# Latent attention: five or six of the sixteen block transfers of a unit issued from GpSimd, the reciprocals widened by a copy and transposed

## What is computed

```python
q = einsum('bld,dhk->blhk', xn, Wq)                 # 16 heads of 64
latent = einsum('bld,dc->blc', xn, Wkv_down)        # 64 wide
k = einsum('blc,chk->blhk', latent, Wk_up)
v = einsum('blc,chk->blhk', latent, Wv_up)
attn = softmax(where(causal, einsum('bqhd,bkhd->bhqk', q, k) / sqrt(64), -inf))
s = einsum('bqhd,hdo->bqo', einsum('bhqk,bkhd->bqhd', attn, v), Wout)
out = x + s * silu(two_layers(xn))
```

## Time and profile before

| | us |
|---|---|
| median of 3 runs | 2399.08 (2394.21 to 2402.8) |
| the profiled execution | 2381.4 |
| its span | 2379.5 |
| TensorE busy in the span | 2109.0 |
| VectorE busy | 1710.9 |
| ScalarE busy | 1339.7 |
| GpSimd busy | 999.0 |

### The profile page before, as it was taken

The page is one execution under the profiler, slowest core; times in us unless marked ns, Lnnn a source line. Parts: engine busy times, 40 slices in busy tenths (PEclk is TensorE's granted clock), DMA queues, the critical chain, the costliest instruction groups (busy, mean ns, idle before and its releaser), DMA issues. The chain is left out here.

```text
span 2379.5 us, 46754 instructions
## 1 busy us (share of the span) xinstructions
PE 2109.0 (89%) x16256; PEld 1663.6 (70%) x16256; DVE 1710.9 (72%) x3004; ACT 1339.7 (56%) x3178; POOL 999.0 (42%) x1081
## 2 busy tenths in 40 slices
PE   6579999999899899999998789888988898898986
PEld 4467777777677677777776667767766776776764
DVE  5587776777777977677763477786778687867783
ACT  3346666766466656666563565555554655455542
POOL 2475666656665657656562223112221222123211
PEclk8789999999899999999998899999999999999998
DMA  8343333333333433333323056775768666867675
GB/s 278 93 106 81 89 94 92 85 82 93 92 92 84 109 95 85 76 77 95 96 71 100 23 136 165 184 185 135 176 173 189 157 166 158 195 145 181 163 186 130
DMA packets 191589, 298.29 MB, mean 125 GB/s; under 512 B 52264, under 2 KB 97660, under 8 KB 190332
## 3 DMA queue, kind: packets, MB, share of 16 engines
q1 hardware_dynamic: 179068, 271.17, 45.2%
q10 hardware_dynamic: 12288, 24.13, 4.1%
HBM read 56.04 MB, written 20.97 MB: 32 GB/s over the span
## 5 line engine op out<-in xcount | busy, mean ns | idle before, releaser
L854 ACT ACTIVATE l_pp<-ps,l_mx 128x256 f32<-128x256 f32 (+1 forms) x512 | 228.4, 463 | 168.1 <-DVE l_mx L991 168.1
L2034 POOL TENSOR_TENSOR g_ctxu<-g_ctxu 128x256 f32<-128x256 f32 (+1 forms) x96 | 88.0, 917 | 550.9 <-ACT g_ctxu L1879 550.7
L1754 PE MATMUL ps<-g_turned,g_latV 128*64 128x256 f32 (+1 forms) x1984 | 289.0, 435 | 0.0
L1858 ACT ACTIVATE g_pt<-ps,g_mx 128x256 f32<-128x256 f32 (+3 forms) x256 | 200.9, 796 | 120.6 <-DVE g_mx L1952 71.1
L1858 ACT ACTIVATE g_pp<-ps,g_mx 128x128 f32<-128x128 f32 (+3 forms) x256 | 173.6, 688 | 166.3 <-DVE g_mx L1957 64.1
L1130 POOL TENSOR_TENSOR l_pp<-l_pp,l_rl 128x1024 f32<-128x1024 f32 (+1 forms) x128 | 230.1, 1798 | 87.4 <-DVE l_rl L999 87.2
L1981 DVE STREAM_TRANSPOSE g_bt<-g_pt 128x1024 f32<-128x1024 f32 (+1 forms) x176 | 191.6, 1123 | 59.5 <-DMA g_turned<-g_bt 39.7
L1754 PEld LDWEIGHTS ps<-g_turned,g_latV 128*64 128x64 f32 x1984 | 154.9, 146 | 74.1 <-issue 33.9
L1147 POOL TENSOR_TENSOR l_act_lo<-l_u,l_act_hi 114x512 fp32r<-114x512 f32 x96 | 126.1, 1314 | 163.0 <-ACT l_act_hi L904 162.8
L991 DVE CUSTOM_DVE_ANT_0 ps<-ps,l_mask 128x256 f32<-128x256 f32 (+1 forms) x512 | 188.4, 441 | 7.4 <-PE ps L703 7.4
L109 PE MATMUL ps<-l_h_hi,l_w_hi 128*114 128x512 f32 (+1 forms) x384 | 160.1, 417 | 25.8 <-DVE l_h_lo L1048 22.0
(11 more groups left out here) (200 smaller groups left out, 6211.1 us busy)
## 6 DMA issues: line engine op xcount, KB each, us to landing
l_pt<-l_bt SPq DMA_DIRECT2D x1024, 64.0 KB, 2.0
g_turned<-g_bt SPq DMA_DIRECT2D x320, 128.0 KB, 3.4
g_turned<-g_bt SPq DMA_DIRECT2D x320, 96.0 KB, 2.2
g_turned<-g_bt SPq DMA_DIRECT2D x224, 112.0 KB, 2.4
g_turned<-g_bt SPq DMA_DIRECT2D x224, 80.0 KB, 2.1
l_tab<-turns SPq DMA_DIRECT2D x64, 128.0 KB, 2.1
g_turned<-g_bt ACTq DMA_DIRECT2D x64, 128.0 KB, 4.4
g_turned<-g_bt SPq DMA_DIRECT2D x96, 64.0 KB, 2.0
```

Source lines behind the costliest of these rows:

```text
L854: act.activation(PP[:, i % NP, at, 0:n], ps[:, bank + a, jj * 2 * P:jj * 2 * P + n], ACT.Exp, bias=mx[:, g % 2, h, at:at + 1], scale=-1.0, ...
L1754: last = pe.matmul(o, latV[:, b % 2, c, :], turned[:, :, a, c, :, :], start=(c == 0), stop=(c == t), skip_group_check=True)
L1858: act.activation(to, both(k, a) if plan.apart(k) else scored(k, a)[0], ACT.Exp, bias=mx[:, u % 2, at:at + 1], accum_out=sm[:, u % 2, at:at ...
```

## The change

Three things are done, and then the order is planned anew.

1. A new table `BELOW` gives five transfers of a short unit and six of a long one to GpSimd, with semaphores sub0 and sub1 of their own. `ASIDE` (ScalarE) is two everywhere. So SyncE issues 9 of 16 in short tiles (12 before) and 8 of 16 in long ones (14 before).
2. `spread`, new on GpSimd, copies the reciprocals, each repeated 64 times, to the second half of `ctxu`, which is 256 or 512 columns. `weigh` transposes that half into PSUM, 2 or 4 transposes of 128x128, in place of the products with the identity. `share` waits for the spread two units back instead of the weighing.
3. All ranks and costs of the planner are new, so that all queues can come out in another order.

```diff
     LONG = NT // 2
-    ASIDE = (((0, 0), (1, 1), (2, 2), (3, 3)),) * LONG + (((0, 0), (1, 1)),) * (NT - LONG)
-    COST = (4.571, 3.923, 2.011, 2.809, 4.828, 5.535, 2.542, 5.643)
+    ASIDE = (((0, 0), (1, 1)),) * LONG + (((0, 0), (1, 1)),) * (NT - LONG)
+    BELOW = (((2, 2), (3, 3), (0, 1), (1, 2), (2, 3)),) * LONG + (((2, 2), (3, 3), (0, 1), (1, 2), (2, 3), (3, 0)),) * (NT - LONG)
+    COST = (2.709, 3.092, 3.306, 2.466, 4.391, 5.098, 3.285, 1.763)
     RANK = {
-        "pe": {"latent": -60.62, "values": -57.85, "query": -30.8, "scores": -17.92, "weigh": 10.13, "wout": 40.53,
-              "back": -13.38},
-        "act": {"split_x": -33.79, "latent": -163.61, "values": -36.79, "query": -27.04, "exp": 14.02, "evacuate": 14.31,
-              "gate": -17.61, "move": 17.17},
-        "dve": {"latent": -51.51, "query": -45.74, "largest": 6.21, "share": -103.46, "blocks": 19.74, "gate": 42.39,
-              "back": -18.9},
-        "pool": {"split_x": -49.69, "divide": 23.65},
-        "sp": {"xn": -39.07, "f": 41.91, "x": 19.24, "move": 22.1, "store": 39.09},
+        "pe": {"latent": -44.66, "values": -28.5, "query": 20.57, "scores": -25.24, "weigh": 9.27, "wout": 61.39,
+              "back": 36.22},
+        "act": {"split_x": -26.65, "latent": -41.17, "values": -25.91, "query": -23.27, "exp": -3.03, "evacuate": 3.82,
+              "gate": 49.96, "move": 8.11},
+        "dve": {"latent": 28.05, "query": -45.43, "largest": 9.61, "share": -17.89, "blocks": 22.83, "gate": -18.32,
+              "back": -21.63},
+        "pool": {"split_x": -50.02, "spread": -7.48, "divide": 22.69, "move": -19.14},
+        "sp": {"xn": -10.42, "f": -2.92, "x": 46.91, "move": 12.22, "store": 56.03},
     }
...
         if kind == "weigh":
             t = self.units[n][1]
             some = 1 if t == 0 else (t + 2) // 2 if event[2] == 0 else t + 1 - (t + 2) // 2
-            return 0.1 + some * (0.44 if t >= self.LONG else 0.91) + (0 if event[2] else 0.11 * self.size(n))
+            return 0.1 + some * (0.44 if t >= self.LONG else 0.91) + (0 if event[2] else 0.055 * self.size(n))
+        if kind == "spread":
+            return 0.25 + 0.00085 * self.size(n) * DH
         if kind in ("evacuate", "divide"):
             return (0.00166 if engine == "act" else 0.0051) * self.size(n) * P / 2 + (0.15 if engine == "act" else 0.55)
         if kind == "move":
-            aside = len(self.ASIDE[self.units[n][1]])
-            return 0.635 * (aside if engine == "act" else 16 - aside)
+            aside, below = len(self.ASIDE[self.units[n][1]]), len(self.BELOW[self.units[n][1]])
+            return {"act": 0.65 * aside, "pool": 0.53 * below, "sp": 0.635 * (16 - aside - below)}[engine]
...
                 if lead and event[2] == 0:
-                    out += [("sp", ("move", u - 2)), ("act", ("move", u - 2))]
+                    out += [(some, ("move", u - 2)) for some in ("sp", "act", "pool")]
         elif kind == "share":
             k = self.first[n + 1] - 1
-            out += [("act", ("exp", k, self.wide(self.units[n][1]) - 1))]
-            out += [("pe", ("weigh", n - 2, 1 if self.units[n - 2][1] else 0))] if n >= 2 else []
+            out += [("act", ("exp", k, self.wide(self.units[n][1]) - 1))] + ([("pool", ("spread", n - 2))] if n >= 2 else [])
+        elif kind == "spread":
+            out += [("dve", ("share", n))] + ([("pool", ("divide", n - 2))] if n >= 2 else [])
         elif kind == "move":
             k = self.first[n + 1] - 1
             out += [("dve", ("blocks", k, 1 if self.long(k) else 0))]
             out += [("pe", ("weigh", n - 2, 1 if self.units[n - 2][1] else 0))] if n >= 2 else []
         elif kind == "weigh":
             b, t, r = self.units[n]
-            out += [("sp", ("move", n)), ("act", ("move", n)), ("act", ("values", (b * NT + t) // TZ)), ("dve", ("share", n))]
+            out += [(some, ("move", n)) for some in ("sp", "act", "pool")] + [ ("act", ("values", (b * NT + t) // TZ)), ("pool", ("spread", n))]
...
+        def below(u):
+            return sum(len(plan.BELOW[units[v][1]]) for v in range(u % 2, u + 1, 2))
+
         def moved(u):
-            return 16 * (u // 2 + 1) - kept(u)
+            return 16 * (u // 2 + 1) - kept(u) - below(u)
...
                     for i in range(4):
                         for j in range(4):
-                            if (i, j) not in plan.ASIDE[units[u][1]]:
+                            if (i, j) not in plan.ASIDE[units[u][1]] + plan.BELOW[units[u][1]]:
                                 sp.dma_start(PT[32 * j:32 * j + 32, u % 2, i, 0:run(u)],
                                              BT[32 * i:32 * i + 32, u % 2, j, 0:run(u)]).then_inc(s[f"pt{u % 2}"], 16)
...
                     if i == 0:
                         pe.wait_ge(s[f"pt{u % 2}"], 16 * moved(u))
                         pe.wait_ge(s[f"own{u % 2}"], 16 * kept(u))
+                        if below(u):
+                            pe.wait_ge(s[f"sub{u % 2}"], 16 * below(u))
                         pe.wait_ge(s["v"], tile(u)[0] + 1)
-                        pe.wait_ge(s["rl"], u + 1)
+                        pe.wait_ge(s["spread"], u + 1)
                         n = plan.size(u) // 2
-                        for h in range(2 * n):
-                            at = bank * CH + (n + h // 2) * P
-                            pe.matmul(flat[64 * (h % 2):64 * (h % 2) + 64, at:at + P], rl[:, u % 2, h:h + 1].to_broadcast([P, DH]),
-                                      ident[:, :], start=True, stop=True, skip_group_check=True)
+                        for j in range(n, 2 * n):
+                            at = bank * CH + j * P
+                            pe.transpose(flat[:, at:at + P], ctxu[:, u % NCU, j * P:(j + 1) * P], ident[:, :])
...
                 def share(u):
                     dve.wait_ge(s["ex"], heads[first[u + 1]])
                     if u >= 2:
-                        dve.wait_ge(s["pv"], u - 1)
+                        dve.wait_ge(s["spread"], u - 1)
                     own = slice(0, plan.size(u))
                     dve.reciprocal(rl[:, u % 2, own], sm[:, u % 2, own]).then_inc(s["rl"], 1)
...
                     if u >= 2 and p == 0 and a == 0:
                         dve.wait_ge(s[f"pt{u % 2}"], 16 * moved(u - 2))
                         dve.wait_ge(s[f"own{u % 2}"], 16 * kept(u - 2))
+                        if below(u - 2):
+                            dve.wait_ge(s[f"sub{u % 2}"], 16 * below(u - 2))
...
+                def spread(u):
+
+                    pool.wait_ge(s["rl"], u + 1)
+                    if u >= NCU:
+                        pool.wait_ge(s["clo"], u - NCU + 1)
+                    if u == 0:
+                        pool.wait_ge(s["cut"], 4)
+                    n = plan.size(u)
+                    pool.tensor_copy(ctxu[:, u % NCU, n * DH:2 * n * DH].rearrange("p (h d) -> p h d", h=n),
+                                     rl[:, u % 2, 0:n].unsqueeze(2).to_broadcast([P, n, DH])).then_inc(s["spread"], 1)
+
...
+                def move(u):
+
+                    pool.wait_ge(s["blocks"], heads[first[u + 1]])
+                    if u >= 2:
+                        pool.wait_ge(s["pv"], u - 1)
+                    for i in range(4):
+                        for j in range(4):
+                            if (i, j) in plan.BELOW[units[u][1]]:
+                                pool.dma_start(PT[32 * j:32 * j + 32, u % 2, i, 0:run(u)],
+                                               BT[32 * i:32 * i + 32, u % 2, j, 0:run(u)]).then_inc(s[f"sub{u % 2}"], 16)
+
                 for e in plan.program["pool"]:
```

More of the change, by code:

```diff
@@ L1233, in __init__ @@
             events[kind] = [(kind, z) for z in range(Z)]
-        for kind in ("evacuate", "divide", "move"):
+        for kind in ("evacuate", "spread", "divide", "move"):
             events[kind] = [(kind, u) for u in range(U)]
@@ L1272, in rank @@
             return self.start[n] + at
-        if kind in ("share", "weigh", "evacuate", "divide", "move"):
+        if kind in ("share", "spread", "weigh", "evacuate", "divide", "move"):
             return self.start[self.first[n + 1] - 1] + at
@@ L1544, in attend_g @@
         tri = ctxu[:, 0, 0:4 * P].rearrange("p (k n) -> p k n", k=4)
-        late = "x_in f_in silu clo latlo v qlo ex ev wo prod back y out".split()
+        late = "x_in f_in silu clo latlo v qlo ex ev wo prod back y out sub0 sub1".split()
         past, last = ({n: sem for n, sem in s.items() if (n in late) == some} for some in (False, True))
@@ L2047, in _ @@
                         forget(pool, over)
+                    elif e[0] == "spread":
+                        spread(e[1])
                     elif e[0] == "divide":
                         divide(e[1])
+                    elif e[0] == "move" and plan.BELOW[units[e[1]][1]]:
+                        move(e[1])
                 pool.wait_ge(s["clo"], len(units))
@@ L2081, in build @@
```

(2 more changed lines are left out.)

## The result

The changed kernel takes 2428.28 us in the median (2423.44 to 2431.25, 4 runs), the kernel before 2397.23 (2394.21 to 2402.8, 4 runs): a ratio of 1.0125, with a 95% interval of 1.0098 to 1.0152. It is slower by 1.25%; I had forecast 2337, faster by 2.6%.

The account below looks back on a forecast made before the run. It took SyncE's issuing queue, beside TensorE, to bound the last stage. Terms 34 + 12 + 27 + 4 - 15 = 62 us less, carried over to the 2399.1 us median, gave 2337 us, range 2285 to 2400.

Parts of the forecast that it names:

- SyncE's queue as the bound: Last stage: SyncE's issuing, 93% occupied, bounds beside TensorE; with fewer issues it falls under 60% and stops being a bound.
- the loop is 7.9 to 8.6 us: Last stage: a long unit's SyncE issues plus landing take this long after the change, shorter than any unit time.
- rival B: Tiles 6 and 7: the DMA engines bound units at their present 11 us, only other units gain; 2363 us, chance 0.17.
- The order planned anew: Queue orders under new ranks: effect unreadable from the trace, taken as 0 with plus or minus 15 us.
- TensorE's work, 42 less 8 us: Weigh: 256 transposes replace 1024 products, saving 42 us, less 8 us not of use in tiles 6 and 7: 34.
- The waits for transfers, 27 us less: TensorE before weigh: 27 of the 37.6 us of waiting for landed transfers would go.
- VectorE's waits: VectorE: most of 32.1 us at the share reciprocal and 45.4 us before g_bt goes; 12 us counted through score banks.
- rival D: GpSimd's queue: its issues cost far more than SyncE's, filling it from about 1.24 us each; 2447 us at 1.4, chance 0.15.
- the 15 us that I charged for a busy GpSimd: GpSimd's queue: 15 us added for pieces of TensorE's work that find it busy, some 0.15 us in each of 96 units.
- Rival C: Last stage: idle time only moves, GpSimd's queue replaces SyncE's as what weigh awaits; 2399 us, no change, chance 0.08.
- rival A: Last stage: the forecast itself, SyncE's queue no longer a bound, TensorE nearer its own work; 2337 us (2285 to 2375), chance 0.60.

Follow-up runs that it names:

- e8: The changed kernel with only its planner told the measured SyncE time of a move by tile and a landing of 3.2 us: 2356.1 us, ratio 0.9846.
- e14: The whole change with measured planner prices and a second set of newly searched ranks: 2324.4 us, ratio 0.9689 to the kernel before.
- e6: The kernel before with half the columns of each block sent from unit 24 on, same number of issues: 2376.21 us, ratio 0.9921.
- e15: The kernel before with measured planner prices and newly searched ranks and spacing: 2366.1 us, ratio 0.9865.

## Why the prediction was wrong, point by point

*SyncE's queue as the bound.* The step that failed is "a long unit takes 8 x 0.69 = 5.5 us of queue", and with it "the loop is 7.9 to 8.6 us". In the medians over batches 1 to 3, SyncE's eight issues for a unit of tile 7 stretch over 7.9 us, and the first product comes 11.4 us after the first issue; in e8 and e14, whose orders don't wait for it so much, 12.5 and 13.6. Until the last block has landed it is 10.3 us in tile 6 and 10.7 in tile 7. As the price of one issue on a queue that issues nearly alone, 0.69 us was right, as e6 shows (0.66 and 0.68 us with half the bytes). I carried it over to three queues at once, where the bytes bound the unit and the slot becomes 1.02 and 1.10 us. The rows had a better estimate for tile 7: 195 GB/s at a busy share of 0.83 make 235 GB/s, at which 2.10 MB take 8.9 us, and with the shortest landing of 1.8 us 10.7 us. This is an estimate, and for tiles 4 to 6 it is too low: 7.4, 8.5 and 9.6 us, where 9.1, 10.3 and 10.3 were measured. In rival B I gave such a bound 0.17. For the kernel before it is not true, since with half the bytes e6 has hardly shorter units there. In the changed kernel the bytes do bound a unit's arrival, but not its time at 11 us, as B had it: e14, with the same transfers in another order, takes 82.7 us for eight units of tiles 6 and 7, 10.3 us each, where the changed kernel takes 90.6. My own sign for B, a DMA share that stays at 85% while the unit time stays at 11 us, came true by half: a unit takes 11.3 us, but the share falls to 0.71.

*The order planned anew, 0 with plus or minus 15 us.* This is the step that turned the sign. I treated the order as a part by itself, to be good or bad by some us. But the plan is made from prices, and the change alters the price of a move: from 11.4 us to 7.6 in a long unit, by a formula that stood in the diff, while the blocks of tile 7 came 11.2 us after the start of a move. The runs give 72 us for the prices of the move, 56 of them for the arrival alone. The plan put `weigh` where the short price seemed to allow it, and in TensorE's in-order queue that became a wait.

*TensorE's work, 42 less 8 us.* The instructions saved 32 to 34 us and not 42 (the transposes take 52.4 or 49.8 us instead of 41.7), but the clock took it: 913.6 us of busy time in the changed kernel, 872 in e14. That waits make the work that follows them dearer was no term of my sum, though the earlier trace rows has it: 0.90 in the last stretch, where TensorE is least busy.

*The waits for transfers, 27 us less.* They became 49.9 us, and most likely the 25.8 beside them. My signs went with them: the chain has 24.0% in SyncE's issues and not under 10, TensorE is idle for 90.1 us before `weigh` and not under 12, and for some 155 us from the first transfer on, not 70. *VectorE's waits*: those in L1977 fell to 16.0 from 32.1, as forecast; those before g_bt rose from 45.4 to 68.7, and 77.2 us for late scores came in. *L1731* fell from 40 to 28 us, which gained nothing, as TensorE stood elsewhere.

*GpSimd.* 0.50 us for an issue against 0.6 taken, so rival D, which ended on the right side, had the wrong reason; its point, 1.24 us, was never near. Of the 15 us that I charged for a busy GpSimd, the 16.0 us of L1977 and 6.1 of TensorE before L1757 are the trace, about as sized.

*Rival C*, engines that wait for each other, comes nearest: the saved work is lost again in waits. But what is waited for is the transfers, not GpSimd. The forecast number itself is met by the change with right prices and searched ranks (2340, 2324); that is luck, as by e15's control only a part of it is the change's own.

*The range.* By its own terms the slow end of rival A is 34 + 12 + 10 + 4 - 15 - 15 = 30 us below 2399, 2369 and not 2375. Nothing hangs on it, as the time lies outside either way.

## What to carry to other kernels

Before taking work off an issuing queue, divide a batch's bytes by the rate that the DMA engines would reach if they were always busy, and add the landing. Here that is 10.7 us for the largest unit, and this, not the shorter queue, sets when its blocks are there. When orders come from a planner, a change to who does what also changes what the planner believes; check each new price against a row: an arrival held up to 3.6 us too early cost 56 of 72 us here, one 3 us too late 30 us, and the change itself is worth 26 to 42 at best. Compare two versions of such a kernel only after both orders have been made with right prices.

## What the runs showed of the hardware that I had not expected

An issue's duration on a queue that competes with others isn't a constant: SyncE's slot for the same transfer was 1.08 us with three queues at full size and 0.65 us with half the bytes, while GpSimd's stayed at 0.50 us (489 to 703 ns over 544). For blocks of 128 KB, landing took longer after GpSimd's issues than after SyncE's; for those of 80 KB it took 3.8 us after either (page part 6 of after: line's transfer, queue, count, KB, median us):

```profile
g_turned<-g_bt SPq DMA_DIRECT2D x200, 128.0 KB, 4.4
...
g_turned<-g_bt POOLq DMA_DIRECT2D x136, 128.0 KB, 5.3
```

And through the granted clock, waits also cost time after their end: behind waits of 1.63 and 2.05 us, 16 products took 3.37 us at a clock of 0.56 instead of 1.95 at 1.00. Why the plan's own span stays 55 to 65 us below the measured stage even at measured prices (951.9 against 1007 for e8, 901.4 against 966 for e14; 903.3 against 1078 for the changed kernel, with its own prices) was not followed further, beyond the price of the move.
